# A gated Mamba cross-attention block with a ternary FFN: the scan's input product in halves through PSUM, delta broadcast by DMA, a ring of four banks, and an FFN pipeline with other lags

## The reference, cut to what matters

```python
x = x + tanh(g_xattn) * ssm(ctx, z=layernorm(x))          # x: (4, 512, 512), ctx: (4, 512, 256)
x = x + tanh(g_ffn) * ffn(layernorm(x))

def ssm(hidden, z, ...):                                   # per batch b; DI=512 channels, NS=16 states, L=512
    u = silu(conv1d_causal(in_proj_w @ hidden, width 4) + conv_b)
    dt_lo, Bm, Cm = split(x_proj_w @ u)                    # 16 + 16 + 16 rows
    delta = softplus(dt_proj_w @ dt_lo + dt_proj_b)
    for t in range(L):                                     # the scan along the free axis
        state = state * exp(delta[t] * A) + delta[t] * u[t] * Bm[t]
        y[t] = sum_n(state[:, n] * Cm[t, n])
    return (y + D * u) * silu(z)

def linear_bit(x, w, g):                                   # int8 rows times ternary weights
    return act_quant(rmsnorm(x) * g) @ ternary(w).T
ffn = lambda x: linear_bit(silu(linear_bit(x, w1, g1)) * linear_bit(x, w2, g2), w3, g3)   # hidden size 2048
```

## Time and profile before

| | |
|---|---|
| median of 3 runs | 878.03 us |
| profiled execution, its span | 881.37 us, 879.1 us |
| DVE busy | 780.2 us (89%), 746 instructions |
| POOL busy | 658.3 us (75%), 242 instructions |
| PE busy | 630.7 us (72%), mean granted clock 0.837 |
| ACT busy | 543.6 us (62%) |
| DMA | 51.25 MB, q1's packets 18.3% of 16 engines |

### The profile page before, as it was taken

How to read it: one execution, slowest core, us unless ns; L and a number is a source line. 1 busy time by engine, 2 the same in 40 slices (tenths; PEclk the granted TensorE clock), 3 DMA queues, 4 the chain that set the end, 5 groups by cost and what they waited for, 6 DMA issues and landing times.

```text
span 879.1 us, 7586 instructions
## 1 busy us (share of the span) xinstructions
PE 630.7 (72%) x2354; PEld 248.4 (28%) x2354; DVE 780.2 (89%) x746; ACT 543.6 (62%) x783; POOL 658.3 (75%) x242
## 2 busy tenths in 40 slices
PE   5575655857867685878768586958686776858996
PEld 3211122323323221223223232313132222314443
DVE  2497979999999999999999999999999999968874
ACT  4586844766553765766749394746666574726773
POOL 1047776565776779796979899796979797986652
PEclk9767675988777887988879788989788787779999
DMA  3594530256320000032000000032000000000000
GB/s 92 116 333 164 214 108 12 100 155 191 132 78 18 12 1 12 0 112 60 13 8 16 0 25 0 16 107 61 12 13 12 13 12 1 12 13 13 13 25 36
DMA packets 26262, 51.25 MB, mean 58 GB/s; under 512 B 6720, under 2 KB 9280, under 8 KB 24048
## 3 DMA queue, kind: packets, MB, share of 16 engines
q1 hardware_dynamic: 26224, 50.78, 18.3%
HBM read 46.32 MB, written 4.46 MB: 58 GB/s over the span
## 4 chain that ended last, share of the span: by engine, by line
POOL 44%; DVE 29%; PE 11%; issue 11%; DMA 2%; ACT 1%; SPq 1%; DVEq 0%; POOLq 0%
POOL hb L526 14%; DVE hb L874 13%; POOL h L496 10%; POOL delta L469 7%; DVE hb L866 7%; POOL a L484 4%; DVE h L1098 3%; PE ring L1238 3%; POOL a L482 3%; PE dl_ps L1209 2%; PE du_ps L1216 2%; POOL zsc L530 2%; POOL yz L490 1%; POOL fsc L504 1%; PE ring L1290 1%
## 5 line engine op out<-in xcount | busy, mean ns | idle before, releaser
L526 POOL TENSOR_TENSOR hb<-hb,c_rep 128x2048 f32<-128x2048 f32 x64 | 294.8, 4606 | 162.1 <-DVE hb L874 147.5
L874 DVE TENSOR_TENSOR_SCAN hb<-dA,hb 128x2048 f32<-128x2048 f32 x64 | 345.2, 5393 | 4.0
L641 ACT ACTIVATE dA<-dl_ps,a_neg 128x511 f32<-128x511 f32 x256 | 154.6, 688 | 122.5 <-PE dl_ps L1209 114.1
L866 DVE TENSOR_TENSOR hb<-du_ps,b_rep 128x2048 f32<-128x2048 f32 x64 | 146.2, 2284 | 13.9 <-PE du_ps L1216 12.8
L1209 PE MATMUL dl_ps<-delta,sel_q 128*128 128x512 f32 x128 | 85.9, 759 | 101.1 <-POOL delta L469 83.7
L1227 PE MATMUL y_ps<-hb,sel_s 128*32 128x512 f32 x512 | 132.1, 663 | 11.5 <-POOL hb L526 11.5
L496 POOL TENSOR_TENSOR h<-h,g3b 128x1024 f32<-128x1024 f32 x32 | 116.6, 3645 | 21.1 <-ACT work L701 21.1
L1216 PE MATMUL du_ps<-du,sel_q 128*128 128x512 f32 x128 | 93.5, 822 | 39.4 <-DVE hb L866 36.6
L1238 PE MATMUL ring<-w1T,a12T 128*128 128x512 fp8e4 x256 | 72.5, 409 | 24.4 <-DVE delta L846 15.3
L649 ACT ACTIVATE h<-ring,deq 128x512 f32<-128x512 f32 x64 | 43.2, 680 | 57.3 <-PE ring L1238 57.0
L1238 PE MATMUL ring<-w2T,a12T 128*128 128x512 fp8e4 x256 | 70.2, 399 | 0.0
(11 more groups left out here) (130 smaller groups left out, 998.5 us busy)
## 6 DMA issues: line engine op xcount, KB each, us to landing
h<-in_L_ffn_w_dram SPq DMA_DIRECT2D x24, 1024.0 KB, 5.3
xt<-in_x_dram SPq DMA_DIRECT2D x16, 256.0 KB, 2.7
b_rep<-bc_scratch SPq DMA_DIRECT2D x16, 256.0 KB, 4.5
c_rep<-bc_scratch SPq DMA_DIRECT2D x16, 256.0 KB, 4.8
x<-in_x_dram SPq DMA_DIRECT2D x4, 1024.0 KB, 8.5
out_dram<-x SPq DMA_DIRECT2D x16, 256.0 KB, 2.0
ctx_nat<-in_ctx_dram SPq DMA_DIRECT2D x4, 512.0 KB, 5.3
g3b<-in_L_ffn_g_dram SPq DMA_DIRECT2D x1, 1024.0 KB, 12.1
```

The source lines that it names most:

```text
L526: g.tensor_tensor(hb[:, s % 4, :, :], hb[:, s % 4, :, :], c_rep[:, :, :], ALU.mult)\
L641: ins = a.activation(dA[:, s % 2, i, 1:L], dl_ps[:, 1:L], ACT.Exp, scale=a_neg[:, s % 16, i:i + 1])
L866: v.tensor_tensor(hb[:, s % 4, :, :], du_ps[:, :].unsqueeze(1).to_broadcast([P, NH, L]), b_rep[:, b % 2, :, :], ALU.mult).then_inc(dbu_don ...
L874: v.tensor_tensor_scan(flat, dA[:, s % 2, :, :].rearrange("p a l -> p (a l)"), flat, 0.0, ALU.mult, ALU.add).then_inc(scan_done, 1)
```

## The change

- **Input product and scan in halves.** `add_input` now makes 2 x 512 elements at a time and writes them to a PSUM pair `dbu_ps` (two banks) instead of `hb`; the scan reads its second operand there and writes `hb`. Each step has two products and two scans of 1024 elements, and `exp_done`, `dbu_done`, `scan_done` count halves. A product waits for the scan of the half before, which reads the same banks.
- **Delta by DMA.** `bcast_delta` leaves PE; SP issues four DMAs of 32 x 512 per step from `delta` to a double buffer `dl_rep` in SBUF, two steps ahead, and `exps` reads that. `bcast_du` contracts over 32 rows instead of 128.
- **Skip term.** D*u enters `y_ps` as one more matmul with a diagonal matrix (`skip_term`); `gated_y` on DVE multiplies `y_ps` by silu(z); `skip`, `add_skip` and POOL's product go.
- **Ring.** `dl_ps` is gone, `dbu_ps` takes two banks, so the ring has `NB` = 4.
- **FFN lags.** A tile is started in the fourth block after its own (`LAG_F` = 4), its second half and everything up to `down` are in the next block (`LAG_G` = 5), and `output` in the first step of the one after (`LAG_O` = 6). `h` holds one tile instead of two. Four tiles (and half of tile 11) are left for the tail, whose loop takes one tile after the other: four chunks of `gate_up`, then hidden transposes and `down` of the tile before.
- **Others.** `u` is a ring of six, computed five blocks ahead; POOL's product with C for step s comes one step later in its order; ACT switches its function tables once per block (to silu and back) instead of twice; the magnitude pass takes two chunks in each of steps 0 to 5, the ternary pass is in steps 7 to 18, its two chunk buffers are `h` and a third of `x1`.

```diff
 KQ = B * ET
-LAG_A, LAG_B, LAG_C, LAG_D, LAG_E = 4, 5, 6, 7, 8
-FIRST = KQ - LAG_C
-NB = 5
+NT = B * L // P
+LAG_F, LAG_G, LAG_O = ET, ET + 1, ET + 2
+TAIL = KQ - LAG_F
+NB = 4
 XB = 3
+UB = ET + 2
...
                                  scratch[b, NS + NH * lo:NS + NH * (lo + 1), :].partition_broadcast(32))\
                       .then_inc(ld_c, 16)
 
+            def bcast_delta(s):
+
+                k, q = divmod(s, Q)
+                if q == 0:
+                    sp.wait_ge(delta_done, k + 1)
+                if s >= 2:
+                    sp.wait_ge(exp_done, 2 * (s - 1))
+                for lo in range(4):
+                    sp.dma_start(dl_rep[32 * lo:32 * lo + 32, s % 2, :], delta[32 * q:32 * q + 32, k % 2, :])\
+                      .then_inc(ld_dl[s % 2], 16)
+
             def load_x1(b):
...
+            def times_c(s):
+
+                pool.wait_ge(scan_done, 2 * (s + 1))
+                if s % 16 == 0:
+                    pool.wait_ge(ld_c, 64 * (s // 16 + 1))
+                g.tensor_tensor(hb[:, s % 4, :, :], hb[:, s % 4, :, :], c_rep[:, :, :], ALU.mult)\
+                 .then_inc(hc_done, 1)
+
+            def z_rstd(k):
...
-            def add_input(s):
+            def add_input(s, half):
 
                 b = s // 16
-                dve.wait_ge(du_bc, s + 1)
-                if s % 16 == 0:
-                    dve.wait_ge(ld_b[b % 2], 64 * (b // 2 + 1))
-                if s >= 4:
+                if half == 0:
+                    dve.wait_ge(du_bc, s + 1)
+                    if s % 16 == 0:
+                        dve.wait_ge(ld_b[b % 2], 64 * (b // 2 + 1))
+                if s + half >= 1:
+                    dve.wait_ge(scan_done, 2 * s + half)
+                v.tensor_tensor(dbu_ps[:, :, :], du_ps[:, :].unsqueeze(1).to_broadcast([P, 2, L]),
+                                b_rep[:, b % 2, 2 * half:2 * half + 2, :], ALU.mult).then_inc(dbu_done, 1)
+
+            def scan(s, half):
+
+                dve.wait_ge(exp_done, 2 * s + half + 1)
+                if half == 0 and s >= 4:
                     dve.wait_ge(sum_done, (s - 4) // 2 + 1)
-                v.tensor_tensor(hb[:, s % 4, :, :], du_ps[:, :].unsqueeze(1).to_broadcast([P, NH, L]),
-                                b_rep[:, b % 2, :, :], ALU.mult).then_inc(dbu_done, 1)
-
-            def scan(s):
-
-                dve.wait_ge(exp_done, s + 1)
-                dve.wait_ge(dbu_done, s + 1)
-                flat = hb[:, s % 4, :, :].rearrange("p a l -> p (a l)")
-                v.tensor_tensor_scan(flat, dA[:, s % 2, :, :].rearrange("p a l -> p (a l)"), flat, 0.0,
+                dve.wait_ge(dbu_done, 2 * s + half + 1)
+                v.tensor_tensor_scan(hb[:, s % 4, 2 * half:2 * half + 2, :].rearrange("p a l -> p (a l)"),
+                                     dA[:, s % 2, 2 * half:2 * half + 2, :].rearrange("p a l -> p (a l)"),
+                                     dbu_ps[:, :, :].rearrange("p a l -> p (a l)"), 0.0,
                                      ALU.mult, ALU.add).then_inc(scan_done, 1)
 
             def evac_magic(job, dst, signal):
...
+                ahead = k + AHEAD < KQ
                 for q in range(Q):
                     s = Q * k + q
-                    add_input(s)
-
+                    add_input(s, 0)
+                    if q == 0 and o >= 0:
+                        output(o)
                     if q == 1 and k >= 1:
-                        add_skip(k - 1)
-                    if q == 2 and ftc >= 0:
-                        ss = square_total(ftc)
-                        hidden_max(ftc, 0)
-                    scan(s)
-                    if q == 0 and fte >= 0:
-                        output(fte)
+                        gated_y(k - 1)
+                    if q == 2 and g >= 0:
+                        max0 = hidden_max(g, 0)
+                    if q == 3 and f >= 0:
+                        quant_scales(f)
+                    scan(s, 0)
                     if q == 0:
-
                         dve.wait_ge(ld_xt[k % 2], 16 * (k // 2 + 1))
                         st = mark(v.bn_stats(zst[:, :], xt[:, k % 2, :]))
-                        if nxt:
-                            taps = mark(conv_tap(b + 1, et, 1))
+                    if q == 2 and f >= 0:
+                        row_bias(f)
+                    if q == 3 and g >= 0:
+                        evac_hT(g)
+                    add_input(s, 1)
+                    if q == 0:
+                        if g >= 0:
+                            mul_up(g, 0)
                         after(st)
                         st = mark(v.bn_aggr(zmv[:, :], zst[:, :]))
-                        if nxt:
-                            after(taps)
...
                     for s in (2 * p, 2 * p + 1):
                         q = s % Q
                         ins = mm(y_ps[32 * q:32 * q + 32, :], sel_s[:, :], hb[:, s % 4, i, :],
-                                 start=(i == 0), stop=(i == NH - 1))
+                                 start=False, stop=(i == NH - 1))
                 ins.then_inc(sum_done, 1)
+
+            def skip_term(k):
+
+                if k == 0:
+                    pe.wait_ge(diag_done, ET)
+                if k >= 1:
+                    pe.wait_ge(yz_done, k)
+                pe.wait_ge(u_done, k + 1)
+                mm(y_ps[:, :], diag_d[:, k % ET, :], u[:, k % UB, :], start=True, stop=False).then_inc(skip_mm, 1)
 
             def gate_up(ft, c):
                 if ft == 0 and c == 0:
-                    pe.wait_ge(wT_done, 4 * WCH)
+                    pe.wait_ge(wT_done, 4 * 8)
                 pe.wait_ge(aT_done, ft + 1)
                 for m, (name, w) in enumerate((("gate", w1T), ("up", w2T))):
                     dst, done = take((name, ft, c))
@@ -1251,22 +1317,23 @@
                                else chunk_buf(c)[:, i, P * t:P * (t + 1)])
 
             ctx_transpose(0)
-            for et in range(ET):
...
                 for q in range(Q):
                     s = Q * k + q
-                    more = s + 1 < Q * KQ
-                    if q == 0 and nxt:
-                        in_proj(b + 1, et)
-                    if q < 3:
-                        bcast_delta(s + 1)
                     if q == 0:
+                        if g >= 0:
+                            gate_up(g, 2)
                         bcast_du(s + 1)
+                        if g >= 0:
+                            gate_up(g, 3)
                         if k >= 1:
                             sum_states(2 * k - 1)
-                        if ftc >= 0:
-                            gate_up(ftc, 2)
-                            gate_up(ftc, 3)
-                        transpose_w(s)
...
                             bcast_du(s + 1)
-                        transpose_w(s)
-                        if ftd >= 0:
-                            down(ftd)
-                        if et == ET - 1 and b + 2 < B:
-                            ctx_transpose(b + 2)
+                    transpose_w(s)
+                    if q == 3:
+                        if f >= 0:
+                            transpose_rows(f)
+                        if g >= 0:
+                            down(g)
+                        if f >= 0:
...
+            last = TAIL - 1
+            gate_up(last, 2)
+            gate_up(last, 3)
             sum_states(2 * KQ - 1)
-            for ft in range(FIRST, KQ + 1):
-                if ft < KQ:
-                    gate_up(ft, 2)
-                    gate_up(ft, 3)
-                transpose_hidden(ft - 1)
-                if ft == FIRST:
-                    transpose_yz(KQ - 1)
-                if ft + 1 < KQ:
+            transpose_yz(KQ - 1)
+            transpose_hidden(last)
+            down(last)
+            transpose_rows(TAIL)
+            for ft in range(TAIL, NT):
+                for c in range(4):
+                    gate_up(ft, c)
+                if ft > TAIL:
+                    transpose_hidden(ft - 1)
+                    down(ft - 1)
+                if ft + 1 < NT:
                     transpose_rows(ft + 1)
-                    gate_up(ft + 1, 0)
-                    gate_up(ft + 1, 1)
-                down(ft - 1)
+            transpose_hidden(NT - 1)
+            down(NT - 1)
 
 
 # ---- launch: one core; inputs and outputs as the reference has them ----
```

751 lines of the change are left out of this document (387 added, 364 removed).

## The result

The changed kernel takes 939.4 us (median of 4, 930.7 to 939.7) against 878.0 for the kernel before. Over all runs of both the ratio is 1.067, 95% interval 1.062 to 1.071 (of the two medians alone it is 1.070). It is slower, as forecast, but by 61 us, not by 17, and outside the range of 848 to 922. The profiled execution spans 936.7 us; TensorE's mean granted clock is 0.774 of full speed, before it was 0.837.

The account below looks back on a forecast made before the run. The prediction saw POOL (44%) and DVE (29%) relieving each other on the chain of waits. 879.1 + 1 - 2.2 + 7.7 + 10.5 = 896.1 us for the profiled span, 895 as the median; range 848 to 922.

Parts of the forecast that it names:

- DVE's own work: Middle blocks: halved products and steady PSUM scans bring a block from 47.2 to 43.8 us before new waits.
- Blocks 6 to 15, +7.7: Middle blocks, first product of block 6 to last scan: 481 us against 473.3, new waits outweighing DVE's savings.
- The three places: DVE's new waits on PE in a middle block: 2.8 us at `output`, 0.5 at `mul_up`, 1.7 for `sum_states`.
- My 2.8: Middle blocks: DVE's forecast wait at `output` for `down`, 2.8 us a block.
- The rival on the clock: PE's stream has more holes and runs at the low clock in blocks and tail: 920 us; chance 0.12.
- Blocks 0 to 5, -2.2: Early blocks: 77 us for blocks 0 and 1, 142 for 2 to 4, 45.7 for 5; 264.7 against 266.9.
- the head at +1: Start to first product: delta for step 0 waits for DMAs, partly offset by a shorter product; bounds -1 and +4.
- Delta late: Steps 0 to 19: chunk loads and SP's waits delay delta's DMAs and `exps`, 2 us each: 935; chance 0.06.
- Tail, +10.5: Behind the last scan: four tiles, one after the other, take 109 us against 98.5.
- The serial chain: Tail: each tile's chain through five engines is longer than their work, 17.8 us to the next gate, before 13.
- the way in: Tail: from the last scan to the first gate of tile 12, forecast 29.2 us.
- DVE as the bound, faster: Rival: PE and ACT run ahead and cover the waits, DVE stays the bound; set at 850 us; chance 0.26.

Follow-up runs that it names:

- e_fill_only: Changed kernel with idle matmuls in two of PE's waits (steps 2 and 3) of blocks 5 to 15, nothing else; 917.7 us.
- e_head: Changed kernel with only the first loads reordered: step sizes ahead of the C operand, some other loads moved into the loop; 931.8 us.
- e_tail: Changed kernel with only the order behind the last scan changed, on all engines; 914.6 us.
- e_warm: Changed kernel with idle matmuls behind the last scan, ahead of the transposes and each row tile's down projection; 934.8 us.
- e_all_ch3: Changed kernel with output, gated_y, exps, first loads and tail reordered, 40 idle matmuls at the end and a third chunk buffer; 859.3 us.
- e_fill: e_all_ch3 plus idle matmuls in two of PE's waits of each block from block 5 on; 845.9 us.
- e_sbuf: Changed kernel with the input product written in halves to SBUF and read there by the scan, instead of PSUM; 1016.8 us.

## Why the prediction was wrong, step by step

- *DVE's own work.* Right by the instruction: 2.28 and 1.22 us against 2.27 and 1.21, and steady. By the block it was some 0.8 us too much (419.7 us without the waits in blocks 6 to 15, against 428). POOL is no bound, right.
- *Blocks 6 to 15, +7.7.* Came as +13.3. The three places were right; that the sum is so near is in part luck. I gave `down` 3.62 us although the same rows showed that PE's first passes after a wait take double, and though I had the broadcast ahead of it at the low level. It takes 4.8 on average over ten blocks. No block is as I had it: where all three are low (2.0 for the broadcast, 1.0 for the transposes, some 5.5 for `down`) `output` waits 4.5, where all are high (1.1, 0.6, 3.62) it waits 1.3. My 2.8 lies between, and so does the mean, 3.1. `gated_y` waits 1.7 each, as forecast; `mul_up` 0.9 against 0.5, softplus 0.5 against 0.3, the evacuation to hT 0.4 against nothing. All waits together are 66.9 us against 53, and the 8 us too much of DVE's own work make up for more than half of that. e_fill_only puts `down` back to 3.62 and gets 1.9 us a block. The rival on the clock was no rival but part of the sum: 21.7 us, with a chance of 0.12 for 25.
- *Blocks 0 to 5, -2.2.* Came as +21, 23.3 over the forecast; this is the step that failed most, and what it had wrong is waits that it put at nothing. In blocks 0 and 1 (88.3 us against 77) I had counted 2 us of waits; DVE waits 16.0: 4.6 at `gated_y`, 4.0 at the weight sum, 3.7 at the first scan, 3.6 in two places at softplus. The first scan and the first softplus (3.1) wait for step sizes queued behind other loads; e_head takes the first away, the second it hands to the first weight chunk. I had priced those DMAs at nothing "after the head" and the head at +1, looking only at when the first product starts. The scan behind it was late. "Delta late" had the mechanism, but not over 20 steps: ACT waited for `dl_rep` in three places, 12.3 us in all. In blocks 2 to 4 (149.2 against 142) the chunks had been seen, and cost 18.4 us against about 22 in the sum; not in the sum were 4.9 at `gated_y` and 1.4 at softplus, and DVE's own work is 124.6 against some 120. In block 5 (50.4 against 45.7) `mul_up` waits 5.3 us in two places, against 0.5.
- *Tail, +10.5.* Came as +22. The serial chain was there as described (e_tail takes 20.5 us of the tail away), and the mis-sized term is PE's durations in it, taken at the upper level of the clock: the way in is longer by 4.3 us, of which 2.7 is `down` (6.35) and 1.0 the transposes; the later tiles by 2.1 and 1.4, where gate groups take 1.9; the end by 3.5, where `down` takes 6.44 and the transposes 2.07. In e_warm 2.8 us of the way in and 1.3 of tile 14 do come off when these fall.
- *DVE as the bound, faster* (0.26, 850). Wrong for this kernel. Its time is near that of e_all_ch3 and e_fill (859 and 846), the same change with another order and, in e_fill, idle matmuls.

The sum of misses: 0.3 head, 23.3 early blocks, 5.6 middle, 11.4 tail, 40.6 us, the distance from 896.1 to 936.7. Two small slips in the prediction's readings change nothing: POOL's product in rows 3 ends at 526.8, not 527.0, and blocks 6 to 15 before took 473.2 us. What stays open is how much of blocks 0 and 1 is PE's pace at the weight sum (4.0 us), which no run took apart.

## What to carry to other kernels

Feeding one operand of VectorE's scan from PSUM kept it from being held up by GpSimd's products and was worth 77 and 93 us here; price such a relief and the order it needs apart, since the time does not show the relief while hand-offs cost more. Removing one wait may show only the next one: ask what is late behind it (here the decays behind `gated_y`, 14.4 of 16.8 us). Matmul durations behind an idle stretch must be taken from rows behind an idle stretch. And a forecast of waits has to be made for the first blocks too, not only for the steady ones: more than half of the miss lay there.

## What the hardware showed that I had not expected

- A scan of two SBUF operands and GpSimd's products both pay for running side by side: the scan goes from 2.25 us at its shortest up to 6.38 in e_sbuf (90 us in all), and GpSimd's short product L504 from 1.27 to 2.99 on average (its engine is busy for some 73 us more).
- Idle matmuls whose results nobody reads keep TensorE at its upper level more of the time (granted clock 0.774 to 0.817) and make a kernel faster (21.7 us alone, 13.4 on top of all else), if they end before the wait does; e_warm's last 50 reached 5.1 us past it, and that end came out 1.3 us longer.
- Four SBUF-to-SBUF copies of 64 KB a step land in 2.0 us in the median. In the first steps they were late (11.4 us at the longest) for the queue ahead of them: with other loads moved behind, ScalarE's waits for them fall from 12.3 to 2.3 us.
